# Attention and FFN on one core: TensorE's units alternate between small pieces and the V products of two units

## The reference

```python
x = x + attn(layernorm(x))      # 16 heads of 8 channels
x = x + ffn(layernorm(x))       # 128 -> 384 -> 128

# attn: q, k, v = x @ W + b, each layer-normalised over the 8 channels of a head
scores = jnp.einsum('bqhd,bkhd->bhqk', q, k) * HD ** (-0.5)
probs = jax.nn.softmax(scores, axis=-1)
out = jnp.einsum('bhqk,bkhd->bqhd', probs, v).reshape(b, s, NH * HD)
return out @ Wo + bo
# ffn: int32 weights times 1/127
h = jax.nn.silu(gate) * up      # gate, up: 128 -> 384
return jnp.einsum('bsh,dh->bsd', h, wd)
```

## Time and profile before

| what | value |
|---|---|
| timed runs, median of 3 | 424.87 us (424.13 to 425.54) |
| profiled execution | 423.12 us, span 421.4 us, mean granted clock 0.951 |
| PE busy | 377.4 us (90% of the span) |
| ACT busy | 288.2 us (68%) |
| DVE busy | 240.7 us (57%) |
| POOL busy | 47.4 us (11%) |

### The profile page before, as it was taken

How to read it: one execution, slowest core, us unless ns; L and a number is a source line. 1 busy time by engine, 2 the same in 40 slices (tenths; PEclk the granted TensorE clock), 3 DMA queues, 4 the chain that set the end, 5 groups by cost and what they waited for, 6 DMA issues and landing times.

```text
span 421.4 us, 7237 instructions
## 1 busy us (share of the span) xinstructions
PE 377.4 (90%) x2383; PEld 154.7 (37%) x2383; DVE 240.7 (57%) x607; ACT 288.2 (68%) x322; POOL 47.4 (11%) x65
## 2 busy tenths in 40 slices
PE   4763899699999999899999999899989999999956
PEld 4533122043342533343343434253334434322445
DVE  4797108048935695459825893569645891244054
ACT  2301699587778787877787787868787777997601
POOL 6400002002002200201010200220020201020010
PEclk9756599899999999999999999999999999999989
DMA  3219504900456017600564036600760046500000
GB/s 106 63 47 199 81 0 157 167 5 1 151 103 125 2 60 177 130 10 0 177 126 70 0 114 135 124 0 16 200 129 2 0 150 128 98 2 0 27 1 25
DMA packets 32943, 32.74 MB, mean 78 GB/s; under 512 B 3608, under 2 KB 29848, under 8 KB 32920
## 3 DMA queue, kind: packets, MB, share of 16 engines
q1 hardware_dynamic: 32056, 32.19, 34.1%
q10 hardware_dynamic: 864, 0.26, 0.3%
HBM read 17.76 MB, written 14.68 MB: 77 GB/s over the span
## 4 chain that ended last, share of the span: by engine, by line
PE 60%; DVE 20%; DMA 5%; issue 5%; POOL 4%; ACT 3%; SPq 2%; DVEq 0%; POOLq 0%; ACTq 0%
PE oacc L703 19%; PE scores L689 12%; PE side L670 10%; PE side L614 5%; PE side L677 5%; DVE xn L865 4%; POOL rs L463 3%; DVE x2n L865 3%; PE side L630 3%; ACT probs L559 3%; DMA kst<-parts_dram 3%; PE side L661 2%; DVE stats L856 2%; DVE mv L859 1%; DMA parts_dram<-parts 1%
## 5 line engine op out<-in xcount | busy, mean ns | idle before, releaser
L559 ACT ACTIVATE probs<-scores 128x1024 f32<-128x1024 f32 x256 | 254.9, 1027 | 77.1 <-PE scores L689 74.7
L703 PE MATMUL oacc<-probs,vaug 128*32 128x512 f32 x1024 | 139.3, 617 | 0.5 <-ACT osb L533 0.4
L689 PE MATMUL scores<-qst,kst 50*128 50x512 bf16 x512 | 99.0, 396 | 16.4 <-DMA kst<-parts_dram 10.1
L689 PEld LDWEIGHTS scores<-qst,kst 50*128 50x128 bf16 x512 | 24.3, 93 | 166.3 <-issue 84.3
L461 POOL TENSOR_SCALAR ve<-mv 128x4 f32<-128x4 f32 (+1 forms) x17 | 4.0, 233 | 315.0 <-DVE mv L859 280.4
L703 PEld LDWEIGHTS oacc<-probs,vaug 128*32 128x32 f32 x1024 | 20.4, 109 | 32.6 <-issue 29.0
L1035 DVE TENSOR_TENSOR y<-side,x 128x512 f32<-128x512 f32 x7 | 4.8, 692 | 46.9 <-PE side L677 46.9
L670 PE MATMUL side<-x2T,wgT 128*128 128x512 f32 x42 | 22.7, 623 | 2.3 <-DVE x2T L1012 2.3
L865 DVE TENSOR_SCALAR xn<-x_in,mv,rs 128x128 f32<-128x128 f32 x32 | 17.4, 700 | 11.1 <-POOL rs L463 11.1
L670 PE MATMUL side<-x2T,wuT 128*128 128x512 f32 x42 | 22.9, 627 | 0.0
L677 PE MATMUL side<-wdT,hT 128*128 128x128 f32 x168 | 22.5, 284 | 0.0
(11 more groups left out here) (128 smaller groups left out, 371.3 us busy)
## 6 DMA issues: line engine op xcount, KB each, us to landing
parts_dram<-parts SPq DMA_DIRECT2D x24, 256.0 KB, 2.5
qst<-parts_dram SPq DMA_DIRECT2D x32, 192.0 KB, 4.9
kst<-parts_dram SPq DMA_DIRECT2D x32, 192.0 KB, 5.4
parts_dram<-parts SPq DMA_DIRECT2D x8, 384.0 KB, 2.6
parts_dram<-parts SPq DMA_DIRECT2D x24, 128.0 KB, 2.1
x_in<-in_L_attn_x SPq DMA_DIRECT2D x8, 256.0 KB, 3.5
x_res<-in_L_attn_x SPq DMA_DIRECT2D x8, 256.0 KB, 5.4
out_dram<-y SPq DMA_DIRECT2D x8, 256.0 KB, 2.0
```

The lines of the kernel that those rows point to most:

```text
L559: act.activation(probs[:, kt, 2 * c:2 * c + 2, :], scores[:, 2 * c:2 * c + 2, :], ACT.Exp)\
L689: last = pe.matmul(scores[:, 2 * c + parity, :], kst[r, pair, kt * P:(kt + 1) * P], qst[r, pair, :], start=True, stop=True)
L703: last = pe.matmul(oacc[STRIP * j:STRIP * (j + 1), :], vaug[:, kt, NG * g + j, :], probs[:, kt, j, :], start=first, stop=last_of_half)
```

## The change

TensorE's order within a unit becomes: both score pairs, the unit's pieces, and, in even units only, the V products of the two units before. All pieces move to odd units, up to three in one. The tanhs move to units 11, 12 and 13, the squares to unit 5, var is split into two pieces that share a bank, and DVE does `silu_up(2)` ahead of `divide(i, 0)`. The last turn has the same slots as the others.

```diff
-SIDE = {1: ["a_xT"], 2: ["b_OT1", "a_q"], 3: ["b_onT", "a_k"], 4: ["b_Wo", "a_v"], 5: ["a_var"],
-        6: ["b_x2T"], 7: ["b_g0"], 8: ["a_rq", "a_rk"], 9: ["b_u0", "b_g1"], 10: ["b_u1", "c_OT0"],
-        11: ["b_g2", "b_u2"], 13: ["b_d0"], 14: ["b_d1"]}
-BANK = {"a_xT": 0, "b_OT1": 1, "a_q": 2, "b_onT": 0, "a_k": 1, "b_Wo": 2, "a_v": 0, "a_var": 1,
-        "b_x2T": 2, "b_g0": 0, "a_rq": 1, "a_rk": 2, "b_u0": 1, "b_g1": 2, "b_u1": 0, "c_OT0": 1, "b_g2": 2,
-        "b_u2": 0, "b_d0": 1}
-
-LAST_SLOTS = {6: [], 7: ["b_x2T"], 8: ["b_g0"]}
+SIDE = {1: ["a_xT"], 3: ["b_OT1", "a_q", "a_k"], 5: ["b_onT", "a_v"], 7: ["b_Wo", "a_var0", "a_var1"],
+        9: ["b_x2T", "a_rq", "a_rk"], 11: ["b_g0", "b_u0", "b_g1"], 13: ["b_u1", "b_g2", "b_u2"],
+        15: ["c_OT0", "b_d0", "b_d1"]}
+BANK = {"a_xT": 0, "b_OT1": 1, "a_q": 2, "a_k": 0, "b_onT": 1, "a_v": 2, "b_Wo": 0, "a_var0": 1,
+        "b_x2T": 2, "a_rq": 0, "a_rk": 1, "b_g0": 2, "b_u0": 0, "b_g1": 1, "b_u1": 2, "b_g2": 0, "b_u2": 1,
+        "c_OT0": 2, "b_d0": 0}
+
+SECOND_HALVES = {"a_var1": "a_var0", "b_d1": "b_d0"}
...
-            SQUARES_AT = 4
-            TANH_AT = {"loop": {7: 0, 9: 1, 11: 2}, "last": {8: 0, 9: 1, 11: 2}}
+            SQUARES_AT = 5
+            TANH_AT = {11: 0, 12: 1, 13: 2}
...
-                elif what == "var":
-                    for w in range(2):
-                        pe.wait_ge(qksq_done, 2 * b + w + 1)
-                        for t in range(NT):
-                            o = (w * NT + t) * NH
-                            last = pe.matmul(bank[:, o:o + NH], qk_sq[:, w, t * P:(t + 1) * P],
-                                             group8[:, 0:P:HD], start=True, stop=True)
-                    last.then_inc(var_filled, 1)
+                elif what in ("var0", "var1"):
+                    w = int(what[3])
+                    pe.wait_ge(qksq_done, 2 * b + w + 1)
+                    for t in range(NT):
+                        o = (w * NT + t) * NH
+                        last = pe.matmul(bank[:, o:o + NH], qk_sq[:, w, t * P:(t + 1) * P],
+                                         group8[:, 0:P:HD], start=True, stop=True)
+                    if w == 1:
+                        last.then_inc(var_filled, 1)
...
                     scores_of(i, u, 0)
-                    if u >= 2 or phase != "first":
-                        times_v(i, u - 2)
                     scores_of(i, u, 1)
                     for name in todo:
                         piece(name, phase, i)
+                    if u % 2 == 0 and (u or phase != "first"):
+                        times_v(i, u - 2)
+                        times_v(i, u - 1)
...
                 if behind:
                     silu_up(i - 1, 1)
+                if behind:
+                    silu_up(i - 1, 2)
                 divide(i, 0)
                 if ahead:
                     fill_v(i + 1, 0)
                 if behind:
-                    silu_up(i - 1, 2)
                     result(i - 1)
```

More of the change, by code:

```diff
@@ L60 @@
 PART_DMAS = sum(len(p) for p in PLACES)
-SIDE = {1: ["a_xT"], 2: ["b_OT1", "a_q"], 3: ["b_onT", "a_k"], 4: ["b_Wo", "a_v"], 5: ["a_var"],
-        6: ["b_x2T"], 7: ["b_g0"], 8: ["a_rq", "a_rk"], 9: ["b_u0", "b_g1"], 10: ["b_u1", "c_OT0"],
-        11: ["b_g2", "b_u2"], 13: ["b_d0"], 14: ["b_d1"]}
-BANK = {"a_xT": 0, "b_OT1": 1, "a_q": 2, "b_onT": 0, "a_k": 1, "b_Wo": 2, "a_v": 0, "a_var": 1,
-        "b_x2T": 2, "b_g0": 0, "a_rq": 1, "a_rk": 2, "b_u0": 1, "b_g1": 2, "b_u1": 0, "c_OT0": 1, "b_g2": 2,
-        "b_u2": 0, "b_d0": 1}
-LAST_SLOTS = {6: [], 7: ["b_x2T"], 8: ["b_g0"]}
-SIDE_ORDER = [p for u in range(NU) for p in SIDE.get(u, []) if p != "b_d1"]
+SIDE = {1: ["a_xT"], 3: ["b_OT1", "a_q", "a_k"], 5: ["b_onT", "a_v"], 7: ["b_Wo", "a_var0", "a_var1"],
[5 more added lines that the diff above has]
+SECOND_HALVES = {"a_var1": "a_var0", "b_d1": "b_d0"}
+SIDE_ORDER = [p for u in range(NU) for p in SIDE.get(u, []) if p not in SECOND_HALVES]
 PHASE_PIECES = {
-    "before": ["a_xT", "a_v", "a_q", "a_k", "a_var", "a_rq", "a_rk"],
+    "before": ["a_xT", "a_v", "a_q", "a_k", "a_var0", "a_rq", "a_rk"],
     "first": [p for p in SIDE_ORDER if p[0] != "b"],
@@ L78 @@
 }
-EARLY = ["a_xT", "a_q", "a_k", "a_v", "a_var"]
+EARLY = ["a_xT", "a_q", "a_k", "a_v", "a_var0", "a_var1"]
 def sequence_of(piece, i):
@@ L305, in build @@
         read_out = {"xT": (xnT_done, 1, 0), "q": (qkc_done, 2, 0), "k": (qkc_done, 2, 1), "v": (vc_done, 1, 0),
-                    "var": (hv_done, 2, 0), "rq": (qkn_done, 2, 0), "rk": (qkn_done, 2, 1),
+                    "var0": (hv_done, 2, 0), "rq": (qkn_done, 2, 0), "rk": (qkn_done, 2, 1),
                     "onT": (onT_done, 1, 0), "Wo": (x2_done, 1, 0), "x2T": (x2T_done, 1, 0), "d0": (y_done, 1, 0)}
@@ L566, in turn @@
                         squares(i + 1)
-                    if phase != "first" and u in TANH_AT[phase]:
-                        j = TANH_AT[phase][u]
+                    if phase != "first" and u in TANH_AT:
+                        j = TANH_AT[u]
                         tanh(i - 1, j, side[:, BANK[f"b_g{j}"], :])
@@ L619, in piece @@
                 b = sequence_of(name, i)
-                if name != "b_d1":
+                if name in SECOND_HALVES:
+                    bank = side[:, BANK[SECOND_HALVES[name]], :]
+                else:
                     bank = bank_free(phase, i, name)
-                else:
-                    bank = side[:, BANK["b_d0"], :]
                 if what == "xT":
@@ L726, in _ @@
                 piece(name, "before", -1)
+                if name == "a_var0":
+                    piece("a_var1", "before", -1)
             for name in EARLY:
@@ L742, in turn @@
                         pe.wait_ge(stackB_loaded, 16 * STACK_DMAS * (i + 1))
-                    slots = {**SIDE, **LAST_SLOTS} if phase == "last" else SIDE
-                    here = PHASE_PIECES[phase] + ([] if phase == "first" else ["b_d1"])
-                    todo = [p for p in slots.get(u, []) if p in here and not (phase == "first" and p in EARLY)]
+                    here = PHASE_PIECES[phase] + [p for p, q in SECOND_HALVES.items() if q in PHASE_PIECES[phase]]
+                    todo = [p for p in SIDE.get(u, []) if p in here and not (phase == "first" and p in EARLY)]
                     scores_of(i, u, 0)
-                    if u >= 2 or phase != "first":
-                        times_v(i, u - 2)
                     scores_of(i, u, 1)
@@ L898, in variances @@
                 dve.tensor_scalar(hv[:, 0:2, :, :].rearrange("p w t h -> p (w t h)"),
-                                  side[:, BANK["a_var"], 0:2 * NT * NH], HEAD_EPS, None, ALU.add)\
+                                  side[:, BANK["a_var0"], 0:2 * NT * NH], HEAD_EPS, None, ALU.add)\
                    .then_inc(hv_done, 1)
```

## The result

| | before | changed |
|---|---|---|
| timed runs, median | 424.5 us (423.83 to 425.54) | 482.81 us (478.48 to 484.81) |
| profiled execution | 423.12 us, span 421.4 | 484.81 us, span 483.1 |
| ratio | | 1.136 (95% interval 1.127 to 1.144) |

What follows compares the result with a forecast made beforehand. TensorE, busy 377.4 of 421.4 us, was taken to bound the kernel. Changes over all turns summed to +39.9 us without the clock and +52.9 with it: 476.0 us profiled, 478 for the runs, range 459 to 490.

Steps and rivals of the forecast that it cites:

- Fewer switches: Steady turn: 16 score runs instead of 29 save 1.4 us, V products back to back save 0.2 us.
- The wait for hyx: Unit 9: TensorE idles 5.0 us before rq, as the first hyx comes 5.6 us after x2n.
- The wait for xn: Before the transposes of xn, after unit 1: TensorE idles 3.0 us (0.6 before), since y must wait for d1.
- The stacks: Stack loads for the next turn's scores: no wait counted, 0.4 us a turn if the load takes 5.9 us.
- the walk: Unit-by-unit timing of one steady turn from its first score pair; the next turn begins at 52.2 us instead of 46.1.
- The clock: Lower clock behind new idles costs 1.5 us behind hyx and 0.8 behind xn, 2.3 a turn in turns 2 to 6.
- Turn 0 and the preparation: Turn 0 paced by exps at 1.9 us a unit, stacks for turn 1 later: +1.9 us; preparation 0.
- Turn 1: No y to wait for, so 50.8 us against 46.2: +4.6 us, and 1.5 for the clock.
- The signs: Right: idles near 3 and 5 us, turns near 52 to 55; wrong: kst waits over 0.5 us, turns under 46.
- Faster by the saved switches: Rival: the waits are covered and only saved switches are left; about 410 us, 412 for the runs; chance 0.04.
- One wait alone: Rival: only rq's wait shows, because ln1 of the next sequence gets through otherwise; 459 us; chance 0.07.
- The clock stays up: Rival: both waits come without low clock; 463 us in the profile, 465 for the runs; chance 0.14.

Runs made afterwards that it cites:

- a_rq_apart: The changed kernel with rq and rk moved from unit 9 to unit 11, behind g0; 474.79 us, ratio 1.120.
- c_result: The changed kernel with DVE forming y of a turn behind ln1_stats and ln1_apply of the next turn instead of before; 477.85 us, ratio 1.120.
- d_filler: The changed kernel with ten idle products, output overwritten, ahead of TensorE's wait for hyx in the loop turns; 470.66 us, ratio 1.099.
- g_turn0_old: The changed kernel with the old order in turn 0 alone, a V product between the two score pairs; 480.51 us, ratio 1.133.
- e_group_only: The kernel before with TensorE's new order, but its old slots for pieces, squares and tanhs; 452.98 us, ratio 1.053.

## Why the prediction was right

The mechanism held: two waits of TensorE that the old slots had covered, and low clock behind them. In turns 2 to 6 the three terms can be set against the trace. TensorE was busy 45.1 us a turn and waited 8.8. Of the 45.1, the bare work is 41.4, an estimate: each group at its fastest in these turns, and those behind hyx, which never ran at full clock there, at their price elsewhere (transposes 1.03, scores 0.53, V 1.86). The rest, 3.7, is the clock. So it was 41.4 + 8.8 + 3.7 = 53.9 us, where I had 43.0 + 9.2 + 2.3 = 54.5.

The total is closer than its parts, by luck: work counted too dear and clock counted too cheap nearly cancel, and turns 2 to 6, 2.7 us too long in all, stand against 3.5 us missed in turn 1 and 7.0 us in turn 0 and the preparation.

- **Fewer switches: right, too small.** Two V in a row took 1.86 us, the far end of my bounds, not 1.97 (0.9 us a turn), d0 and d1 together 2.77 in turn 7 (455.61 to 458.38), not 3.08. Runs of four scores took 0.53.
- **The wait for hyx: right.** 5.0 us forecast, 4.3 to 5.0 measured, and a_rq_apart shows it is the slot. The 5.6 us chain is unchanged.
- **The wait for xn: right as a sum.** 3.0 us forecast; 2.05 and the 0.93 us for the stacks are 2.98, because y can start while TensorE waits for kst. c_result shows the cause, and that its removal is worth less than its length.
- **The stacks: a term I had at nothing.** I counted 0 with up to 0.4 a turn; they took 0.8 to 1.2. A wait for them over 0.5 us was on my list of signs that the theory is wrong, and it came. The chain was right (tanh, lower_parts, loads), but in the turn shown it ended later than I had it: the tanh 41.1 us into the turn for 39.3, behind stretches of low clock that this part of the walk left out, lower_parts at 44.4 for 42.6, and from there 10.1 us to the scores for 9.5. TensorE was ready for them at 53.5. Since the wait for xn is shorter by the same time, the sum did not suffer.
- **The clock: right, mis-sized.** 2.3 us a steady turn forecast, 3.7 by the estimate above, from 2.0 to 5.4 in single turns. Behind hyx it cost 1.8 to 3.0 where I took 1.5; d_filler, which takes it out, gained 2.0 to 2.6. Behind xn it cost 1.6 in three of the five turns and nothing in two, where I took 0.8 for each. In the turn shown a third stretch, from 220.54, cost 1.6 more; I had forecast no wait ahead of it and there was none over 0.3 us.
- **Turn 0 and the preparation: the step that failed.** I wrote that turn 0 is "paced by exps at 1.9 a unit" and only rq moves. Two V products in a row break that pace: two units took 4.66 us (78.74 to 83.40 from score pair to score pair), not 3.8. Of the 5.9 us, g_turn0_old gives back 3.2, and 2.7 stay for rq's slot, for which I had 1.9. And the new banks act in the preparation as well, where q now waits for v to be read and v for q:

```profile
15.46 3.78 PE L631 MATMUL side<-xnT,wqkv 128*128 128x512 f32 x4 [0.78 <-DVE v_c L892]
...
35.97 2.07 PE L636 MATMUL side<-wqkv,xnT 128*128 128x128 f32 x8 [1.10 <-DVE qk_c L886]
```

  Together 7.0 us above the forecast. The traces of the experiments tell how much of the preparation's 3.05 us is the tables' doing: the six kernels with the old `SIDE` and `BANK` reach their first scores at 42.5 to 44.8 us, the eight with the new ones at 44.9 to 46.4. That is about 2 us; the rest lies in the spread.
- **Turn 1:** I took the wait for xn as absent there, as y is; it was 2.15 us. ln1_stats of that turn also stands behind the divide of c_OT0, which moved to unit 15: in DVE's timeline that divide waits 9.9 us for the transposes of 87.75, begins at 88.45, and ln1_stats follows at 89.66. c_result, which moves only y, keeps the wait in turn 1 (2.29 us).
- **The signs.** Two at the page's level missed. DVE's wait for d1 before y was to stay long; it fell from 46.9 us in seven turns to 10.5, which follows from d1 standing last in its turn, as in my own walk. ACT's busy time was to stay, and its idle to grow by 6 to 9 us a turn; it was 34.4 us busy for 35.6, and its idle grew by 9.7 (20.2 for 10.5). The others came: the wait for hyx is the longest in sum of TensorE's waits, and turns took 52.6 to 54.8 us.
- **The rivals.** "Faster by the saved switches" fell with the result, and e_group_only shows that even with the old slots the switches do not pay. "One wait alone" fell with the 2.05 us before the transposes of xn; c_result, which has one wait alone, costs 478 and not 459. "The clock stays up" fell with the granted clock of 0.61 behind hyx, and d_filler shows that it is on the path.

## What to carry to other kernels

When small pieces are gathered into one slot, price the chain on the other engine between two of them, not their own length: a piece that another one depends on through that engine needs as much other work between as the chain takes, and a wait taken out may come back at the chain's end. Grouping like work on the bounding engine pays only as long as the engine that it feeds keeps its buffers full; two long products in a row starved it here. Check phases of the program that share the tables (banks, slots) but have another bound, such as the first turn, by their own rows.

## What was not expected of the hardware

The granted clock fell without a long idle. In the changed kernel's turn 0 the longest idle between 76.25 and 83.72 is 0.97 us, and behind that stretch the granted clock is 0.56, most of it at its lower level:

```profile
82.48 0.39 PE L691 MATMUL scores<-qst,kst 50*128 50x512 bf16 x2 [0.96 <-ACT probs L560]
83.40 0.39 PE L691 MATMUL scores<-qst,kst 50*128 50x512 bf16 x2 [0.53 <-ACT probs L560]
83.72 3.33 PE L705 MATMUL oacc<-probs,vaug 128*32 128x512 f32 x16
```

```profile
76.25:83.72 7.47, 4.49 (x37) 1.03 (x33) 2.25 (x3) 6.09 (x7) 0.00 (x0) 1.00 0.73 242
83.72:86.98 3.26, 3.26 (x19) 0.60 (x18) 0.00 (x0) 1.46 (x2) 0.00 (x0) 0.56 0.95 173
```

The kernel before, with six idles of 0.2 to 0.4 us from 53.76 to 75.99 in the same turn, kept 1.00. But short waits are not all of it. In the steady turn shown, the clock also fell at 220.5, where TensorE had been busy 13.3 of the 13.7 us before and the longest idle was 0.29 us:

```profile
206.89:220.54 13.65, 13.34 (x101) 6.78 (x98) 4.42 (x13) 10.50 (x12) 0.00 (x0) 1.00 0.00 0
220.50:224.60 4.10, 4.10 (x23) 0.75 (x25) 3.13 (x11) 1.94 (x2) 2.28 (x3) 0.58 0.00 0
```

In turn 1 the same products with the same idle (0.29 us at 109.58) kept full clock: the V products of 113.22 took 1.85 us. What decides it stays open. The low stretches do not fall in the same place in every turn or run, which goes with the changed kernel's wider spread of times (1.3% against 0.4%).
